# Masked attention in a four-layer network: the vector engine turns the value products straight out of PSUM and, in the second layer, also writes the rows of turned maxima

## What is computed

```python
q = heads(layernorm(x) @ Wq + bq); k = heads(ctx @ Wk + bk); v = heads(ctx @ Wv + bv)
scores = q @ k.T / sqrt(16)                 # 512 x 512 for each of 8 x 16 heads
scores = scores + adj                       # layer 1 only
scores = where(mask, scores, very_negative)
out = softmax(scores) @ v
x = x + out @ Wo + bo
```

## Time and profile before

| | |
|---|---|
| time, median of 3 runs | 3710.58 us (3708.59 to 3712.11) |
| time of the profiled execution | 3708.85 us |
| its span, first to last instruction | 3707.1 us |
| PE busy | 3108.9 us, 84% |
| DVE busy | 2445.2 us, 66% |
| ACT busy | 2237.8 us, 60% |
| POOL busy | 1133.5 us, 31% |
| mean granted clock of TensorE | 0.927 |

### The profile page before, as it was taken

The page is one execution under the profiler, slowest core; times in us unless marked ns, Lnnn a source line. Parts: engine busy times, 40 slices in busy tenths (PEclk is TensorE's granted clock), DMA queues, the critical chain, the costliest instruction groups (busy, mean ns, idle before and its releaser), DMA issues. The chain is left out here.

```text
span 3707.1 us, 67269 instructions
## 1 busy us (share of the span) xinstructions
PE 3108.9 (84%) x17185; PEld 1561.6 (42%) x17185; DVE 2445.2 (66%) x7452; ACT 2237.8 (60%) x3034; POOL 1133.5 (31%) x1290
## 2 busy tenths in 40 slices
PE   5999998787688888759978888888379999975997
PEld 3344432343333333226645555555144434323665
DVE  5777776887677677642226777878867777766431
ACT  2777777664499899941116666677537777761111
POOL 4444440000555565201113333331242312111232
PEclk8999999998899999969988989999589999996998
DMA  5322420000533343110029989997041222102342
GB/s 152 90 73 72 104 68 13 23 1 24 135 98 98 98 117 101 36 53 0 0 66 319 299 278 294 312 318 267 9 100 42 58 59 48 36 32 96 91 102 58
DMA packets 212159, 392.90 MB, mean 106 GB/s; under 512 B 24633, under 2 KB 76985, under 8 KB 211657
## 3 DMA queue, kind: packets, MB, share of 16 engines
q1 hardware_dynamic: 168777, 296.38, 28.8%
q10 hardware_dynamic: 36864, 83.90, 6.1%
q0 software_dynamic: 6144, 8.39, 1.3%
HBM read 189.88 MB, written 96.47 MB: 77 GB/s over the span
## 5 line engine op out<-in xcount | busy, mean ns | idle before, releaser
L506 DVE CUSTOM_DVE_ANT_0 A_sums<-A_ring_ps,A_bias 128x512 bf16<-128x512 f32 x1536 | 1036.0, 687 | 437.2 <-PE A_ring_ps L322 411.8
L569 ACT ACTIVATE A_probs<-A_p_ps 128x1024 f32<-128x1024 f32 x768 | 779.3, 1016 | 199.6 <-PE A_p_ps L337 110.3
L322 PE MATMUL A_ring_ps<-A_k_stack,A_q_stack 96*128 96x512 bf16 x1536 | 574.7, 391 | 101.3 <-DVE A_maxima L506 35.0
L554 ACT ACTIVATE A_p_ps<-A_biasT 128x1024 f32<-128x1024 bf16 (+1 forms) x512 | 525.8, 1027 | 52.4 <-ACT A_m_row L532 7.5
L337 PE MATMUL A_p_ps<-A_q_stack,A_k_stack 99*128 99x512 bf16 x1536 | 465.5, 384 | 40.9 <-ACT A_p_ps L554 35.5
L353 PE MATMUL A_oT_ps<-A_probs,A_v_aug 128*17 128x512 f32 x3072 | 410.9, 607 | 0.5 <-ACT A_probs L569 0.5
L322 PEld LDWEIGHTS A_ring_ps<-A_k_stack,A_q_stack 96*128 96x128 bf16 x1536 | 147.6, 97 | 606.5 <-DVE A_maxima L506 373.7
L1158 DVE CUSTOM_DVE_ANT_0 A_scores<-A_qk_ps,A_rel_in 128x384 f32<-128x384 f32 (+3 forms) x512 | 232.1, 485 | 84.5 <-PE A_qk_ps L1042 76.2
L1065 PE MATMUL A_t_ps<-ident,A_scores 128*128 128x128 f32 x1280 | 226.8, 299 | 56.1 <-DVE A_probsT L1148 46.9
L1213 ACT ACTIVATE A_rel_out<-A_rel_ps 128x1024 f32<-128x1024 f32 (+3 forms) x256 | 180.0, 703 | 145.3 <-PE A_rel_ps L1031 143.6
L1148 DVE COPY A_probsT<-A_t_ps 128x384 f32<-128x384 f32 (+3 forms) x512 | 228.8, 484 | 51.4 <-PE A_t_ps L1065 43.4
(11 more groups left out here) (346 smaller groups left out, 5331.1 us busy)
## 6 DMA issues: line engine op xcount, KB each, us to landing
A_k_stack<-A_parts SPq DMA_DIRECT2D x192, 256.0 KB, 5.1
A_q_stack<-A_parts SPq DMA_DIRECT2D x192, 256.0 KB, 5.5
A_rel_dram<-A_rel_out ACTq DMA_DIRECT2D x64, 512.0 KB, 5.6
A_rel_in<-A_rel_dram SPq DMA_DIRECT2D x64, 512.0 KB, 5.5
A_rel_dram<-A_rel_out ACTq DMA_DIRECT2D x64, 384.0 KB, 5.0
A_rel_in<-A_rel_dram SPq DMA_DIRECT2D x64, 384.0 KB
A_ctxT<-in_ctxT SPq DMA_DIRECT2D x32, 512.0 KB, 6.5
A_mask_in<-in_mask SPq DMA_DIRECT2D x64, 256.0 KB, 4.6
```

The source lines that it names most:

```text
L322: nc.tensor.matmul(bank(*turn)[:, :], q_stack[0:KS, a_par, j * GH + i, t * P:(t + 1) * P], k_stack[0:KS, a_par, j * GH + i, :], start=True ...
L506: nc.vector.tensor_tensor_reduce(out=sums[:, i % NX, :], in0=bank("p1", s * GH + i)[:, :], in1=bias[:, t, :], scale=-1.0, scalar=3.4028235 ...
L554: nc.scalar.activation(p2_ps[half][:, :, :], turned, ACT.Copy).then_inc(seeded, 1)
L569: nc.scalar.activation(probs[:, s % 2 * 2 + half, :, :], p2_ps[half][:, :, :], ACT.Exp).then_inc(exp_done, 1)
```

## The change

- ACT's copy of `oT_ps` is gone, with the tile `oT_sb` and the semaphore `oT_read`. DVE turns `oT_ps` itself, and PE's first value product of the next group waits for that turn (`o_turned`).
- `HEADS` goes from 12 to 10: the turn and the three instructions after it come two positions earlier on DVE.
- In layer 1 alone the rows of turned maxima are copied to `m_row` by DVE, between the two reductions of p = 8j+3, and not by ACT. `DVE_READS` says which kinds of unit DVE reads.

```diff
-        oT_sb = sb("oT_sb", [P, S], F32)
...
+        DVE_READS = ("v", "out", "m") if adj is not None else ("v", "out")
...
-        HEADS = 12
+        HEADS = 10
...
-                            pe.wait_ge(dve_read if k in ("v", "out") else act_read, read_of(b - back, k, n))
+                            pe.wait_ge(dve_read if k in DVE_READS else act_read, read_of(b - back, k, n))
...
             if kb == 0 and later(b * NG + (s - 1) // TPB):
-                pe.wait_ge(oT_read, b * NG + (s - 1) // TPB)
+                pe.wait_ge(o_turned, b * NG + (s - 1) // TPB)
...
-                dve.wait_ge(oT_read, G + 1).then_inc(apart_dve, 1)
-                nc.vector.transpose(o_tok[:, :], oT_sb[:, :]).then_inc(o_turned, 1)
+                dve.wait_ge(pv_done, (G + 1) * TPB * GH).then_inc(apart_dve, 1)
+                nc.vector.transpose(o_tok[:, :], oT_ps[:, :]).then_inc(o_turned, 1)
...
+        def dve_maxima_row(dve, b, n, j):
+
+            k = b * (NG // 2) + j // 2
+            dve.wait_ge(front_full, uses_before(b) + n + 1).then_inc(apart_dve, 1)
+            if later(k):
+                dve.wait_ge(m_placed[j % 2], k * GH * 16).then_inc(apart_dve, 1)
+            nc.vector.tensor_copy(m_row[:, j % 2, :], bank("m", j)[0:GH * 3, :]).then_inc(dve_read, 1)
+            dve.wait_ge(dve_read, read_of(b, "m", j)).then_inc(m_row_ready, 1)
...
+                    if i == pair[0] and "m" in DVE_READS:
+                        for n, kind, k in shared(plan, p):
+                            if kind == "m":
+                                dve_maxima_row(dve, b, n, k)
...
-                if p % 8 == 2 and has(b, s - 2):
-                    G = b * NG + (s - 2) // TPB
-                    act.wait_ge(pv_done, (G + 1) * TPB * GH)
-                    if later(G):
-                        act.wait_ge(o_turned, G)
-                    nc.scalar.activation(oT_sb[:, :], oT_ps[:, :], ACT.Copy).then_inc(oT_read, 1)
```

More of the change, by code:

```diff
@@ L148, in masked_attention @@
         pv_done = sem("pv_done")
-        oT_read = sem("oT_read")
         o_turned, sums_inverted = sem("o_turned"), sem("sums_inverted")
@@ L187, in reads_before @@
         def reads_before(b, kind):
-            alike = [k for k in ("xT", "k", "q", "m", "v", "out") if (k in ("v", "out")) == (kind in ("v", "out"))]
+            alike = [k for k in ("xT", "k", "q", "m", "v", "out") if (k in DVE_READS) == (kind in DVE_READS)]
             def count(units):
@@ L200, in read_of @@
             units = [u[1:] for u in (plan_of(b) if isinstance(b, int) else PLAN)]
-            alike = [u for u in units if (u[0] in ("v", "out")) == (kind in ("v", "out"))]
+            alike = [u for u in units if (u[0] in DVE_READS) == (kind in DVE_READS)]
             return reads_before(b, kind) + alike.index((kind, i)) + 1
@@ L521, in act_shared @@
         def act_shared(act, n, front_ps, kind, i, base, b, par):
-            if kind not in ("xT", "q", "k", "m"):
+            if kind in DVE_READS:
                 return
```

## The result

| | before | changed |
|---|---|---|
| time, median | 3709.59 us (3706.27 to 3712.11, 4 runs) | 3670.38 us (3668.36 to 3679.84, 4 runs) |
| profiled execution | 3708.85 us | 3679.84 us |
| span | 3707.1 us | 3678.1 us |
| mean granted clock of TensorE | 0.927 | 0.925 |

The ratio is 0.990, with a 95% interval of 0.9888 to 0.9913. The forecast was 35 off, 3676 us, with a range of 3660 to 3697. The profiled execution of the change is the longest of its four, so its trace shows 29 us of the 39.

What follows compares the result with a forecast made beforehand. It took ACT (91% busy) to bound layer 1 and PE (97% and 96%) layers 0 and 3. Terms −31 + 0 − 3 − 2 = −36, rounded to −35, took 3710.6 to 3676 us, range 3660 to 3697.

Steps and rivals of the forecast that it cites:

- Layer 1: Layer 1 gains 3.5 us a block, 28 us over 8 blocks, plus 3 us in the last block: −31 us.
- layers 0 and 3: New PE wait, 5.3 and 2.4 us after cover, against 5.4 us of block-start gain per layer: 0 and −3 us.
- all layers' ends: At each masked layer's end the last group's copy and semaphore fall out: −0.7 us, three times, −2 us.
- a late m_row: In layer 1, PE's shared unit waits 0.80 us for m_row on a late ACT; it would start 0.45 us earlier.
- the block start: The turn into heads_outT no longer stands right ahead of the statistics PE waits for: 0.77 us in all masked layers.
- 0.95 for j = 1, 2, 3: Layer 1: gain of 0.95 us in each of a block's groups j = 1, 2, 3; 0.65 at j = 0.
- The new wait on PE: First value products wait for DVE's turn, starting at te + 0.82, te ending p = 2's second reduction: 0.10 to 0.44 us.
- Within 0.3 us: Sign for layers 0 and 3: their block time stays within 0.3 us.
- the signs named: Trace checks, such as layer 1's block falling from 76.1 to about 72.5 us; above 74.5 would show the prediction wrong.
- ACT's whole share arrives: Rival: layer 1 gives 8 × 5.7 = 46 us, sum −51, time 3660 us; chance 0.13.
- PE and DVE take back half: Rival: only 0.45 us a group left, 14 us in layer 1; 3691 to 3704 us; chance 0.22.
- slower: Rival: turn reads PSUM at half rate, 1.25 us, each PE wait 0.54 us longer, sum 0; chance 0.04.

Runs made afterwards that it cites:

- e10: The whole change, unaltered, run again on another chip: 3663.70 us, ratio 0.9896 to the kernel before.
- e2: Kernel before with only m_row moved to DVE in layer 1; ACT's copy of oT_ps and HEADS = 12 stay: 3692.50 us, ratio 0.9947.
- e3: Kernel before with HEADS = 10 instead of 12 and nothing else: 3685.87 us, ratio 0.9927.
- e1: The change without its m_row part, so ACT writes m_row in all layers: 3681.98 us, ratio 0.9915 to the kernel before.
- e8: The change with ACT's copy of oT_ps to SBUF kept, so no turn out of PSUM: 3674.75 us, ratio 0.9897 to the kernel before.
- e12: e8 run again on the same chip as e10: 3674.71 us, ratio 0.9913 to the kernel before.
- e6: The change with each turn made twice, first into an unread spare tile, PE waiting for the second: 3717.52 us, ratio 1.0014 to the kernel before.
- e5: The change with m_row written by DVE in all three masked layers: 3677.42 us, ratio 0.9907 to the kernel before.
- e9: e8 with m_row written by DVE in all three masked layers: 3676.97 us, ratio 0.9922 to the kernel before.
- e11: Kernel before with HEADS = 11 instead of 12 and nothing else: 3693.19 us, ratio 0.9957.

## Why the prediction came out right, step by step

**The total was partly luck.** Layer 1 was forecast as −31 and gave −22.7 us in the products' spans; layers 0 and 3, with what all layers' ends were to give, were forecast as −5 and gave −12.6. The two misses, 8 us each way, cancelled. The mechanism of layer 1 (a late m_row) and that of the block start were right, and so was the choice that not all of ACT's saving arrives.

**Layer 1, block nearly right, shares wrong.** Forecast 3.5 us a block and −31 us; measured 3.24 us a block and −22.7 us (−23.7 in e10). The last block, for which 3 us more were counted, gave 66.55 − 62.19 = 4.4 us against 3.2 of a steady block, so 1.1 more. The third block, the one with DVE's long stops, grew from 81.9 to 83.8 us, which alone is 5 us of the 8 missing. By group of a block (from one start of the value products to the next, same three blocks):

| layer 1 | j = 0 | j = 1 | j = 2 | j = 3 |
|---|---|---|---|---|
| before, us | 20.28 | 17.65 | 20.39 | 18.32 |
| changed | 18.62 | 17.81 | 19.35 | 17.65 |
| gain | 1.66 | −0.16 | 1.04 | 0.67 |
| forecast | 0.65 | 0.95 | 0.95 | 0.95 |
| e2's gain (m_row alone) | 0.84 | 0.00 | 1.00 | 0.90 |
| e3's gain (`HEADS` alone) | 0.94 | 0.03 | 0.00 | 0.00 |

Two steps of the working failed, and their errors cancelled. "0.95 for j = 1, 2, 3" took one place, the v unit of the earlier trace rows, as a sample of all. The group with the out unit hadn't waited for m_row (one wait of 0.4 us in 13 units, above), so there was nothing to give there. And at j = 0 I let the block-start gain stand *in place of* the m_row gain, since DVE was behind there. The two edits alone give 0.84 and 0.94, together 1.78, and the change has 1.66: within what a trace can tell they add up. For j = 2 the size was right, for j = 3 it was 0.3 us too large. One reading was off as well: of the 26.5 us ahead of ACT's seeds, which were to stay, 6.9 were waits behind m_row, which went; 22.9 us are left. The sum for a group had also been rounded up: 0.45 and 0.4 to 0.5 us make 0.85 to 0.95, not 0.9 to 1.0.

**The gain of the earlier turn into heads_outT** was forecast as 0.77 us a block start and measured as 0.96 to 1.19 us (e3). The mechanism was right; the term was too small by about a quarter to a half. What it left out in layers 0 and 3 is the value unit's read behind the old turn, 0.26 us in the block shown under e3.

**The new wait on PE** was forecast as 0.44 us where PE stood ready and 0.10 where it was late. The products start at te + 0.68 to 0.78 and not te + 0.82. The turn starts at the start of the accumulator's short read and not behind it (both at 1298.23), which saves 0.08 us, and PE follows 0.06 us behind the turn's end (up to 0.15 in other groups), where the prediction had set 0.10 from no row. Where PE stood ready its start moves from te + 0.38 to te + 0.68, by 0.30 us, and 0.24 us of it show as idle time. Forecast for the sum of the three layers: 8.4 + 9.5 + 6.2 = 24.1 us over 84 groups; measured on PE's products 12.2 us over 47. The wait was about half as large as set down. In layers 0 and 3 what it takes back shows in the tables: the three kernels with the turn out of PSUM (the change, e1, e10) have 71.58 and 71.36 us a block on average, the three with the copy (e3, e8, e12) 71.13 and 71.10.

**Layers 0 and 3.** Forecast 0 and −3 us. Measured −4.0 and −8.6 in the products' spans, from blocks shorter by 0.44 and 0.90 us. Both terms above erred the same way: the block start gave more, and the wait cost less, by the averages just given 0.46 us a block in layer 0, where 0.76 (5.3 us over 7 blocks) were set down, and 0.26 in layer 3, where it was 0.34. "Within 0.3 us" did not hold.

**Layer ends** were to give 2 us. The last block's span shrinks by 1.1 us in layer 0 (53.94 to 52.84), but by 0.7 in e3 (53.23), where ACT's copy is still there: 0.4 us for the copy, 1.2 us over three layers.

**Of the signs named**, block about 72.5: 73.4, half way to what would have refuted it. ACT about 90%: 89%. PE 90%: 87%. m_row 0.68 us: 0.674. No unit waits for m_row in layer 1: so. The 0.47 us wait behind the statistics: gone. The waits for the turn: 12.2 us on PE's products, under the 40.

**The rivals.** That ACT's whole share arrives would have been 5.7 us a block in layer 1; it was 3.24. That PE and DVE take back half would have left 14 us of layer 1; it kept 22.7. The price of longer waits in "slower" was measured by e6: a turn longer by 0.67 us moves the time by 42 us, where a turn longer by 0.54 us had been worked out as 35, which is 43 for 0.67.

The Trainium skill, "VectorE: DVE Perf Modes", section "The TRN2 errata", would have had the turn out of PSUM an estimated 65 ns longer than the one out of SBUF. The trace has 710 against 707 ns, so for this instruction and this shape the measurement decides: 3 ns. The sum would have lost 6 us by the page.

**Where the gain comes from.** e2 and e3 together, 20 + 27 = 47 us, are a little more than e8's 38 and the change's 37 and 39 (e10); the products' spans say the same, 22.5 + 22.2 = 44.7 against 37.7 in e8. So the gain is that of two edits, m_row on DVE in layer 1 and the heads two positions earlier. Dropping ACT's copy, the part from which one would have expected it (96 × 0.58 = 56 us of ACT's time), brings nothing that these runs can tell from zero. That it is the new wait on PE which takes it back is argued from the blocks of layers 0 and 3 and from e6, not shown for layer 1.

**Open.** e5 and e9 have the shortest blocks of layers 0 and 3 and the shortest products' spans of all, 9 us under the change's and 5 to 6 under e10's, and no shorter time. e11's missing gain in layer 1 isn't explained; its span of that layer is 3.3 us under that of before, e3's 6.6. No version here is measurably better than the change.

## What to carry to other kernels

When an edit has several parts, build each alone: here the part that took the most work off ACT was worth nothing measurable, and a constant that moved four DVE instructions away from two places where PE waits for DVE was worth over half. When DVE in place of ACT frees a PSUM bank that PE refills, PE's wait for it is nearly all time (0.85 us for each us in e6), and placing the read earlier moves the wait on to the reader itself. In a list of who waited, count PE's products and its weight loads apart: added up, they gave 2.7 times the wait that counts. Before multiplying one place of a trace by the number of groups, look at the waits of each kind of unit apart: v, k and q units on the maxima's bank waited 0.71 to 0.86 us, of the out units one, 0.4 us.

## What the runs showed of the hardware

The turn, queued on DVE behind a reduction's accumulator read, starts at the read's start and not 0.08 us later, as the two rows at 1298.23 show; so do 85 of the 96 turns of this trace.

The time of one and the same kernel goes with the granted clock. The four runs of the change:

```
mean granted clock   0.925    0.927    0.928    0.929
time, us             3679.84  3671.89  3668.86  3668.36
```

This is about 3 us for each 0.001. Not every kernel's runs line up so well: e1 has 3681.98 us at 0.930 and 3677.09 at 0.928. The runs of e5 have a mean of 0.924, those of e8 0.924, e9 0.925 and e12 0.926, those of the change 0.927 and e10 0.928. The traces show where: two stretches of layer 2 by windows, first in the changed kernel's trace, then in e10's (granted clock third from the end).

```profile
1900.00:2300.00 400.00, 333.15 (x2866) 207.79 (x2864) 282.66 (x968) 252.50 (x473) 135.52 (x236) 0.90 0.89 288
```

```profile
1900.00:2300.00 400.00, 339.73 (x2964) 212.70 (x2964) 289.34 (x987) 259.61 (x487) 135.84 (x238) 0.92 0.90 293
```

The same code had 0.90 in the one and 0.92 in the other, and was ahead by 98 matmuls in 400 us. Shorter blocks in the masked layers and a lower clock elsewhere would explain why e5 and e9 gain nothing, but these are only runs side by side; that the one causes the other wasn't shown.
